# Both token tiles of every norm on VectorE, with GpSimd keeping sums, splits and residuals

## The reference, cut to what matters

```
h = _layernorm(x) * (1.0 + scale1) + shift1
Q, K, V = h @ Wq + bq, h @ Wk + bk, h @ Wv + bv        # layers 1 and 2 rotate Q and K
attn = softmax(Q K^T / sqrt(8)) @ V
x = x + gate1 * (attn @ Wo + bo)
h = _layernorm(x) * (1.0 + scale2) + shift2
x = x + gate2 * (gelu(h @ W1 + b1) @ W2 + b2)
...
x = x + gate_msa * where(m, fwd(norm) + bwd(norm), 0)  # layer 3, no attention
x = x + gate_mlp * ff_out
```

## Time and profile before

| | |
|---|---|
| Median of 3 runs | 419.15 us (415.48, 419.73, 419.15) |
| The profiled execution's own time | 417.63 us |
| Its span | 415.7 us |
| TensorE, VectorE, ScalarE, GpSimd busy | 93%, 79%, 78%, 45% of the span |
| Mean granted TensorE clock | 0.979 |

### The profile page before, as it was taken

How to read it: one execution, slowest core, us unless ns; L and a number is a source line. 1 busy time by engine, 2 the same in 40 slices (tenths; PEclk the granted TensorE clock), 3 DMA queues, 4 the chain that set the end, 5 groups by cost and what they waited for, 6 DMA issues and landing times. The chain is left out here.

```text
span 415.7 us, 10244 instructions
## 1 busy us (share of the span) xinstructions
PE 388.4 (93%) x3666; PEld 205.8 (49%) x3670; DVE 329.4 (79%) x768; ACT 323.8 (78%) x634; POOL 187.5 (45%) x290
## 2 busy tenths in 40 slices
PE   8699899999999999999999998999999999998996
PEld 3444343455544544554545544545555444435874
DVE  6497999989886499898899874899898889935343
ACT  5207786799898968887989887769797999895664
POOL 4539999525745155453162354171451320004564
PEclk9759999999999999999999998999999999999999
DMA  7700237210005000013000023000050000000001
GB/s 254 184 15 14 78 113 203 72 32 2 2 2 149 7 6 2 2 53 103 3 6 2 2 56 98 6 2 2 2 135 20 3 2 16 2 0 3 2 0 39
DMA packets 17186, 17.63 MB, mean 42 GB/s; under 512 B 2460, under 2 KB 15454, under 8 KB 17120
## 3 DMA queue, kind: packets, MB, share of 16 engines
q1 hardware_dynamic: 15840, 16.19, 13.8%
q10 hardware_dynamic: 1296, 0.79, 0.8%
HBM read 6.62 MB, written 0.52 MB: 17 GB/s over the span
## 5 line engine op out<-in xcount | busy, mean ns | idle before, releaser
L1397 DVE TENSOR_REDUCE mx<-max_ps 128x1 f32<-128x512 f32 x384 | 241.9, 682 | 30.3 <-PE max_ps L908 29.2
L1223 ACT ACTIVATE probs<-exp_ps 128x512 f32<-128x512 f32 x384 | 202.6, 605 | 29.4 <-PE exp_ps L917 28.3
L908 PE MATMUL max_ps<-k_stack,q_stack 64*128 64x512 bf16 x384 | 113.5, 390 | 6.9 <-DMA k_stack<-parts 3.5
L1098 PE MATMUL pv_ps<-probs,v_ones 128*32 128x256 f32 x1536 | 103.0, 385 | 4.5 <-ACT probs L1223 3.8
L917 PE MATMUL exp_ps<-q_stack,k_stack 64*128 64x256 bf16 x768 | 101.3, 271 | 0.6 <-ACT probs L1223 0.5
L1417 POOL TENSOR_SCALAR var_eps<-mv 128x2 f32<-128x2 f32 (+2 forms) x33 | 6.5, 198 | 131.1 <-DVE mv L1257 130.0
L1098 PEld LDWEIGHTS pv_ps<-probs,v_ones 128*32 128x32 f32 x1536 | 41.1, 109 | 42.7 <-ACT probs L1223 17.2
L908 PEld LDWEIGHTS max_ps<-k_stack,q_stack 64*128 64x128 bf16 x384 | 29.4, 93 | 61.9 <-DVE mx L1397 36.2
L917 PEld LDWEIGHTS exp_ps<-q_stack,k_stack 64*128 64x128 bf16 x768 | 43.3, 94 | 29.4 <-ACT probs L1223 11.5
L1235 ACT ACTIVATE mrows<-exp_ps 8x256 bf16<-8x256 bf16 x48 | 17.5, 365 | 17.5 <-PE exp_ps L1083 17.1
L1030 PE MATMUL exp_ps<-hT,w 128*128 128x256 f32 x96 | 29.3, 425 | 0.8 <-ACT hT L1157 0.8
(11 more groups left out here) (128 smaller groups left out, 485.1 us busy)
## 6 DMA issues: line engine op xcount, KB each, us to landing
k_stack<-parts SPq DMA_DIRECT2D x36, 128.0 KB, 2.5
q_stack<-parts SPq DMA_DIRECT2D x30, 128.0 KB
w<-in_w_dram SPq DMA_DIRECT2D x4, 448.0 KB, 3.3
w<-in_w_dram SPq DMA_DIRECT2D x4, 256.0 KB, 2.9
w<-in_ada_dram SPq DMA_DIRECT2D x1, 896.0 KB, 5.2
w<-in_rows_dram SPq DMA_DIRECT2D x1, 832.0 KB, 7.4
q_stack<-mrows SPq DMA_DIRECT2D x48, 4.0 KB
x<-in_x_dram SPq DMA_DIRECT2D x2, 256.0 KB, 3.5
```

Of the source, the lines that this page charges most:

```text
L908: return pe.matmul(max_bank(n), half(q_stack, b, pair, j)[:, t * P:(t + 1) * P], half(k_stack, b, pair, j), start=True, stop=True)
L1098: mm = pe.matmul(pv_ps[32 * j:32 * j + 32, cols_of(g // 2)], v_ones[:, b, kt, 4 * g + j, :], probs[:, (4 * i + j) % RING_P, cols_of(of_two ...
L1223: act.activation(probs[:, tile % RING_P, :], exp_bank(e), ACT.Exp, scale=SCORE_SCALE[hc // 2 // NB]).then_inc(exp_read, 1)
L1397: dve.tensor_reduce(mx[:, G % 2, t, 2 * (pair % 2) + j:2 * (pair % 2) + j + 1], max_bank(n), AX_X, ALU.max, negate=True).then_inc(max_read, 1)
```

## The change

`shared` returns false, so that GpSimd writes no normalised tile: VectorE issues L1321 for both tiles of a half, and TensorE's transposes wait for both by `xhat_ready`. GpSimd keeps the rotary sums, the splits and the residuals. Beside it two numbers of the planner differ: VectorE's lead is 0.85 for 1.15, and the preference of ROWS is -0.6 for -0.8. Since `make_order` also costs XH by `shared` (0.4 on VectorE beside 0.85 on GpSimd where it is shared, 0.8 on VectorE where it is not), the whole list comes out anew from the first layer on.

```
-AHEAD = {"DVE": 1.15, "ACT": 0.1, "POOL": 1.65, "SP": 0.95}
-SLACK = {"ROWS": -0.8, "DENSE": -0.3, "PV": 0.85, "ANG": 0.1, "EXP": 0.1, "MAX": 0.8, "NEAR": 0.15, "BESIDE": 0.5, "ALONE": 0.25, "CHANGE": 0.2, "LAST": 0.4}
+AHEAD = {"DVE": 0.85, "ACT": 0.1, "POOL": 1.65, "SP": 0.95}
+SLACK = {"ROWS": -0.6, "DENSE": -0.3, "PV": 0.85, "ANG": 0.1, "EXP": 0.1, "MAX": 0.8, "NEAR": 0.15, "BESIDE": 0.5, "ALONE": 0.25, "CHANGE": 0.2, "LAST": 0.4}
...
 def shared(norm):
 
-    return norm[1] in (0, 1) and norm[0] >= NB
+    return False
```

## The result

The changed kernel takes 422.74 us (median of 420.63, 421.99, 423.48 and 426.81) against 419.44 us for the kernel before in the same comparison; the ratio is 1.0135 with an interval of 1.0095 to 1.0175. The ratios in this document are made over the fast executions of both kernels in one comparison and are not quotients of the medians; that quotient is 1.0079 here (3.3 us), from four executions of each kernel. The changed kernel is slower by 1.4%, where I forecast no change (419.1 us). Its profiled execution took 420.63 us with a span of 418.5 us; 0.0135 of the median of before is 5.7 us.

What follows compares the result with a forecast made beforehand. In the attention VectorE (89% busy) and ScalarE (87.5%), tied through TensorE's list, were taken to bound; the tail, GpSimd's list. +4.5 - 2.5 - 1.0 + 0.5 = +1.5 us on 417.63 gave 419.1 us, range 413.5 to 424.5.

Steps and rivals of the forecast that it cites:

- VectorE's tiles in the attention: Attention: added L1321 tiles cost 6.4 us of VectorE time, of which 0.7 reaches the end, +4.5 us.
- Layer changes, leads, preferences: First layer change +0.5 us, second -1.0 us, other effects of leads and preferences at zero.
- Tail: After the attention: removed L1491 and a new order shorten GpSimd's chain of waits, -2.5 us, at most 4.0, at least 0.
- the leads and preferences: VectorE's list: less waiting for `rstd` against less time for the maxima's transfer, put at zero, 2 us either way.
- the layer changes: First: later keys' and queries' items, +0.5 us; second: queries directly behind keys, earlier third-layer scores, -1.0 us.
- The wait before the third layer's scores: Second layer change: VectorE's wait of 5.19 us would shrink and bounds the gain, taken as -1.0 us.
- the two rivals: Whole kernel: faster by the new order, 412.4 us, 19%; slower by additions holding up VectorE, 425.6 us, 27%.
- The added tiles: Attention norms: 10 second tiles at 0.5 us beside GpSimd's additions, 5 at 0.28, together 6.4 us of VectorE time.
- the share that is carried: Attention: part of VectorE's added time reaching the end, between 0 and 1, taken as 0.7.
- The wait of 2.58 us for `rstd`: Tail: VectorE's wait behind GpSimd's L1491 would go, as two L1491 before the statistics give 1.65 us.
- The slower one: Attention: additions hold up VectorE at every norm, +9.6 us, tail only -1.65, layer changes 0; 425.6 us, 27%.

Runs made afterwards that it cites:

- Old list: The list of the kernel before kept item for item, but VectorE writes both tiles everywhere; 420.35 us, ratio 1.0054 to the kernel before.
- e15: Before's list, VectorE writes both tiles, and in the attention alone GpSimd's addition L1434 waits until both are written; 418.91 us, ratio 1.0019 to before.
- e16: The changed kernel, and in the attention alone GpSimd's addition L1434 waits until both tiles are written; 422.72 us, ratio 1.0116 to the kernel before.
- e13: The changed kernel with before's list up to exponential 79 and its own list behind it; 422.46 us, ratio 1.0107 to the kernel before.
- e3: The changed kernel with the planner's numbers of before (lead 1.15, ROWS -0.8); 436.11 us, ratio 1.0425 to the kernel before.
- e1: The kernel before with its list kept item for item, but VectorE writes both tiles; 420.35 us, ratio 1.0054 to the kernel before.
- e4: The kernel before, GpSimd keeping its tile, with the list made by the changed numbers (lead 0.85, ROWS -0.6); 431.41 us, ratio 1.028.
- e8: e7 with the residual of tile (7, 3) ahead of the statistics of (7, 0) in GpSimd's list; 416.06 us, ratio 0.9972 to the kernel before.
- e7: Before's list, VectorE writes both tiles only in the six norms behind the last exponential; 416.04 us, ratio 0.997 to the kernel before.
- the spliced lists: Three kernels with lists joined from pieces of before's and the changed list, VectorE writing both tiles; ratios 1.0117, 1.0106 and 1.0107 to the kernel before.
- e9: The changed kernel with the residual of tile (7, 4) ahead of the statistics of (7, 3) in GpSimd's list; 423.55 us, ratio 1.0138 to before.
- e14: Before's list, VectorE writes both tiles in the attention's 19 shared norms only, GpSimd keeps its tile in the tail; 421.03 us, ratio 1.0077 to before.

## Why the prediction was wrong

| Term | Forecast | Old list | Changed kernel |
|---|---|---|---|
| VectorE's tiles in the attention | +4.5 us | +3.0 (292.97 - 289.97) | +1.4 (0.9 as in e15, 0.5 by e16) |
| Layer changes, leads, preferences | -0.5 | 0 | +4.1 (294.95 - 290.86) |
| Tail | -2.5 | -1.2 (38.9 - 40.1) | -0.3 (39.8 - 40.1) |
| Sum | +1.5 | +1.8 | +5.2 |
| Measured, by the ratio | | +2.3 | +5.7 |

**The step that failed is the one on the leads and preferences, "I put the two against each other and at zero, with 2 us either way", with the 0.5 and -1.0 for the layer changes.** The runs showed 4.1 us there in place of -0.5. I costed a list that was new from the first layer on by the two places where I could name a difference. At those places I was partly right. The wait before the third layer's scores, 5.19 us in the earlier trace rows, is

```profile
244.83 0.47 DVE L1340 SCALAR_TENSOR_TENSOR work<-max_ps,vec_qk,rot 128x256 f32<-128x256 f32 x1
245.46 0.48 DVE L1340 SCALAR_TENSOR_TENSOR work<-max_ps,vec_qk,rot 128x256 f32<-128x256 f32 x1 [0.16 <-PE max_ps L878]
...
260.83 5.12 DVE L1397 TENSOR_REDUCE mx<-max_ps 128x1 f32<-128x512 f32 x8 [1.83 <-PE max_ps L908]
```

1.83 us, with the queries directly behind the keys. Yet from the 256th to the 384th exponential the changed kernel takes 107.9 us and before 107.4. At the first layer change the wait of 4.09 us is gone, and VectorE waits 6.36 us for another product of TensorE, that of its sum into x:

```profile
141.79 0.42 DVE L1366 TENSOR_TENSOR x<-max_ps,xg 128x256 f32<-128x256 f32 x1 [6.36 <-PE max_ps L1043]
```

e13 took part of that change back (19.1 us for 21.1, before 18.3) and gained nothing certain by it. Most of the price was elsewhere, in waits between TensorE and its two readers, among which those of ScalarE for `oT` and `mrows` grew most. e15 beside e16 shows its size here, 1%; e3 against e1 and e4 against before show 3 to 4% for other numbers. A range of 2 us for it was too narrow by half or more.

**The median came near the forecast by luck.** 422.74 us lies inside the 413.5 to 424.5 us that I gave, because errors of opposite sign met: the list cost 4.1 us that I had at -0.5, the tiles 1.4 that I had at 4.5. The range was also not what I said of it: half way to the two rivals would have been 415.8 to 422.4, with the median outside.

**The added tiles** were sized well: I had 6.4 us; over the attention's 19 norms a tile or pair occupies VectorE 7.8 us before, 14.3 after, which is 6.5 more. That GpSimd's additions of two operands hold it up, and its tiles don't, held as well. A pair beside two of them took 1.43 us:

```profile
104.03 1.43 DVE L1321 TENSOR_SCALAR xhat<-x,mv,rstd 128x128 f32<-128x128 f32 x2 [0.53 <-POOL rstd L1418]
...
103.97 1.41 POOL L1536 TENSOR_TENSOR work<-work,rot 128x256 f32<-128x256 f32 x2
```

The Trainium skill (SBUF — State Buffer, section Who interferes with whom) has a two-port instruction of VectorE and GpSimd shut each other out; the trace agrees where GpSimd's instruction is such an addition, and not for the tile of the earlier trace rows, which ran beside L1491. What I over-priced was the share that is carried, 0.7: it was 3.0 of 8.1 us in e1 (15.9 for 7.8), 0.9 of 4.6 in e15, and 1.4 of 6.5 in the changed kernel. VectorE at 89% still had places to take them up, for its idle time between exponentials 32 and 384 shrank instead, to 43.9 us in e1 from 48.7 in e8, which has before's attention and, as e1, no fall in it.

**The tail** was the term that I took near its upper end by adding waits that don't add. The wait of 2.58 us for `rstd` is gone (0.46 us, the first row), as forecast. But in the changed list GpSimd and VectorE meet later (VectorE, then GpSimd):

```profile
397.90 0.41 DVE L1321 TENSOR_SCALAR work<-x,mv,rstd 128x128 f32<-128x128 f32 x1 [0.46 <-POOL rstd L1418]
...
406.40 1.37 DVE L1321 TENSOR_SCALAR work<-x,mv,rstd 128x128 f32<-128x128 f32 x2 [0.40 <-DVE x L1363]
...
409.15 0.41 DVE L1321 TENSOR_SCALAR work<-x,mv,rstd 128x128 f32<-128x128 f32 x1 [0.96 <-POOL rstd L1418]
410.12 0.35 DVE L1363 SCALAR_TENSOR_TENSOR x<-max_ps,mask_col,xg 128x128 f32<-128x128 f32 x1 [0.55 <-POOL xg L1432]
...
406.29 1.41 POOL L1434 TENSOR_TENSOR xg<-x,gate_b 128x256 f32<-128x256 f32 x2
```

A pair beside two L1434 takes 1.37 us, the last sum into the single tile (7, 4) starts 31.4 us after the last exponential for 30.4 before, and 0.3 us are left of the 2.5. e7 gives 1.2 with the old list, and e8 shows that little more is to be had there by an earlier residual.

**The rivals.** The slower one named the right sign for a wrong reason: the collisions that e16 takes away are 0.5 us of the changed kernel by its profile, and one of 0.8 us stays in it. What made the kernel slower, the new list, I had listed with a bound, not as a way in which the kernel could go. What stays open is the cause of the 4.1 us within the list: the waits for `oT` and `mrows` are named by the traces, but no run took them away, and the spliced lists left most of the loss in place.

## What to carry to other kernels

Where a planner writes the order, a changed cost or preference can be a new order everywhere, and in the three lists tried here its price was 1 to 4%, which the places named in advance did not show; hold the list fixed and change the engine first, then the list, and price them apart. A tile moved to an engine at 89% cost a fifth to two fifths of its time; that it then starts together with the other engine's two-operand additions cost more than the work with the old list (2.1 us for 0.9), and one wait on the engine with time to spare took that back. Before two profiles are compared to a microsecond, look for falls of the clock in each stretch, and take them off.

## What the runs showed of the hardware

- What a fall of TensorE's clock to the lower level costs differs by place: 1.6 us around exponential 256 (before beside e8, and e9 beside the changed kernel), and 1.6 in the tail (41.7 us in e14 for 40.1), where this row has the fall:

```profile
377.60:391.60 14.00, 12.09 (x74) 8.62 (x74) 6.00 (x24) 6.64 (x15) 4.87 (x10) 0.88 0.00 1
```

  but nothing around 73 us (exponentials 63 to 79 took 19.1 us in e14 with one, 19.1 in e1 without).
- VectorE's tile from one SBUF tile to another takes 0.71 to 0.82 us when it starts with an addition of two operands on GpSimd, for 0.34. When the addition (128x256) is already under way, the tile ends 0.08 us behind it: 0.51 us with 0.43 left (85.66 us in the changed kernel), 0.62 with 0.54 (194.85 us in e1), 0.75 with 0.67 (98.21 us in e1). The reductions out of PSUM keep their median of 0.68 us beside GpSimd's instructions of two operands and alone (85 and 195 of them in the kernel before).
